# A dense expert network: routing weights broadcast by DMA from device memory, rings of three banks, down projection two pairs behind

## What is computed

```python
fs = _grouped_routing_scores(router_scores)            # zero outside the groups chosen
up = jnp.einsum('td,edh->teh', xt, Wup) + bup
gate = jnp.einsum('td,edh->teh', xt, Wgate) + bgate
h = jax.nn.silu(up) * gate * fs[:, :, None]
out = jnp.einsum('teh,ehd->td', h, Wdown) + fs @ bdown
x = _layernorm(x + out)
```

## Time and profile before

| what | us |
|---|---|
| median of the runs (3 runs, lowest and highest) | 5069.64 (5061.39 to 5078.28) |
| span of the profiled execution, first to last instruction | 5066.8 |
| stage 2, `expert_mlps`: from ScalarE's first instruction to VectorE's first sum with x | 536.0 to 767.7 |
| in it, TensorE busy | 81% of the whole span; in 536 to 767 us 205.0 of 231.0 |

### The profile page before, as it was taken

The page is one execution under the profiler, slowest core; times in us unless marked ns, Lnnn a source line. Parts: engine busy times, 40 slices in busy tenths (PEclk is TensorE's granted clock), DMA queues, the critical chain, the costliest instruction groups (busy, mean ns, idle before and its releaser), DMA issues. The chain is left out here.

```text
span 5066.8 us, 77700 instructions
## 1 busy us (share of the span) xinstructions
PE 4085.0 (81%) x29323; PEld 2224.5 (44%) x29323; DVE 3485.7 (69%) x5453; ACT 2507.2 (49%) x3544; POOL 1378.9 (27%) x1033
## 2 busy tenths in 40 slices
PE   5640696999999999999995995866996767888883
PEld 3630234666666666666652332432443332222232
DVE  5579444777777777777784445766773558888868
ACT  2120243666666666666662223543564344677772
POOL 0000300566666666666664303000000100000000
PEclk5565798999999999999997996987997687999996
DMA  0010001000000000000003106316650333323300
GB/s 19 1 60 0 0 0 51 1 14 1 14 1 14 14 1 14 1 14 1 1 1 130 58 0 150 53 15 102 84 77 4 90 59 62 55 48 53 49 3 9
DMA packets 135603, 167.70 MB, mean 33 GB/s; under 512 B 19498, under 2 KB 108092, under 8 KB 134676
## 3 DMA queue, kind: packets, MB, share of 16 engines
q1 hardware_dynamic: 127540, 146.39, 14.3%
q0 software_dynamic: 6528, 16.42, 1.3%
q10 hardware_dynamic: 1184, 0.12, 0.0%
HBM read 125.31 MB, written 34.55 MB: 32 GB/s over the span
## 5 line engine op out<-in xcount | busy, mean ns | idle before, releaser
L3001 POOL TENSOR_TENSOR arena<-arena 128x512 f32<-128x512 f32 (+1 forms) x768 | 1131.7, 1475 | 692.0 <-ACT arena L2957 638.6
L2452 ACT ACTIVATE arena<-ps 128x1024 f32<-128x1024 f32 (+1 forms) x688 | 703.3, 1023 | 333.7 <-PE ps L2377 323.0
L2470 DVE TENSOR_REDUCE arena<-ps 128x2 f32<-128x826 f32 (+1 forms) x576 | 564.9, 981 | 185.3 <-PE ps L2323 177.5
L3017 DVE TENSOR_TENSOR arena<-arena 128x1024 f32<-128x1024 f32 (+1 forms) x448 | 644.9, 1478 | 13.8 <-ACT arena L2984 13.8
L3039 DVE TENSOR_TENSOR arena<-ps,arena 128x512 f32<-128x512 f32 (+1 forms) x768 | 530.4, 691 | 178.5 <-ACT arena L2951 144.4
L2323 PE MATMUL ps<-arena 48*128 48x413 bf16 (+3 forms) x1920 | 436.4, 334 | 135.9 <-DVE arena L2470 67.2
L2951 ACT ACTIVATE arena<-ps 128x1024 f32<-128x1024 f32 (+1 forms) x448 | 410.3, 960 | 205.1 <-PE ps L2879 197.0
L2863 PE MATMUL ps<-arena 128*128 128x256 f32 (+1 forms) x1664 | 444.0, 392 | 20.5 <-DVE arena L3025 19.2
L2957 ACT ACTIVATE arena<-arena 128x1024 f32<-128x1024 f32 (+1 forms) x448 | 425.0, 992 | 50.7 <-DVE arena L3017 48.2
L2396 PE MATMUL ps<-arena 128*9 128x256 f32 (+2 forms) x5504 | 436.2, 389 | 10.5 <-ACT arena L2440 7.7
L2879 PE MATMUL ps<-arena 64*128 64x256 f32 (+1 forms) x3328 | 427.3, 391 | 5.5 <-ACT arena L2973 1.3
(11 more groups left out here) (647 smaller groups left out, 5810.8 us busy)
## 6 DMA issues: line engine op xcount, KB each, us to landing
arena<-ctx_parts SPq DMA_DIRECT2D x96, 200.1 KB
arena<-ctx_parts SPq DMA_DIRECT2D x192, 100.1 KB
arena<-in_ctx_feat SPq DMA_DIRECT2D x8, 1601.0 KB, 6.4
arena<-in_ctx SPq DMA_DIRECT2D x16, 768.0 KB
arena<-diff_att_stack SPq DMA_DIRECT2D x60, 192.0 KB
ctx_parts<-arena SPq DMA_DIRECT2D x24, 400.2 KB, 3.8
arena<-in_w SPq DMA_DIRECT2D x1, 6416.0 KB, 18.3
arena<-in_ctx_feat SPq DMA_DIRECT2D x8, 800.5 KB
```

The costliest lines, as they stand in the source:

```text
L2452: act.activation(self.prob[0:rows, u % 3, :], self.ps[0:rows, 2 * (u % 2):2 * (u % 2) + 2, :].rearrange("p n c -> p (n c)"), ACT.Exp).then ...
L2470: ins = dve.tensor_reduce(dst[:, :, j // 2], self.ps[:, 4:6, 0:hi - lo], AX.X, ALU.max)
L3001: pool.tensor_tensor(acc[0:rows, u % 2, :], before, sc[0:rows, u % 2, t, :], ALU.add).then_inc(added, 1)
L3017: dve.tensor_tensor(e, e, mb[0:rows, u % 2, None, :].to_broadcast([rows, n, 2 * S]), ALU.subtract).then_inc(sub_done, 1)
```

## The change

It touches only stage 2.

- `expert_scores`: SyncE waits for `mask_ready` and stores `fs` (64 x 2,048 f32, 0.5 MB) to a scratch tensor `fs_rows` in device memory (new line 1038).
- `expert_mlps`: SyncE loads, for each block n and each chunk c of two pairs, the 8 experts' rows of `fs_rows`, each repeated over 32 partitions, into a buffer `share` [128, 16, 512]: four DMAs per chunk (one per 32 partitions, 2 rows of 2 KB for each partition), 128 in all. Those of block 0 wait for the store alone; each later chunk waits until the same chunk of the block before has been read (`gw_ready`).
- The spread product, the spread matrix in the weight slab, GpSimd's splits and ScalarE's pass over the gate bank are gone. VectorE's first instruction is now a `scalar_tensor_tensor`, (gate bank + bias) * share, straight from PSUM.
- Up and gate have rings of three PSUM banks, and `silu`, `gw` and `hid` three buffers (`RING0 = 3`). The down product stands two pairs behind, and two banks (6, 7) take the sums of alternating blocks.
- The loops over n are unrolled; ScalarE copies the sum of block n-1 after the third Silu of block n, and the turn of the first three blocks no longer waits for the copy of the fourth.

```diff
-WEIGHTS[2] = [... ("bdown", E0, D), ("spread", FB, MT0 * P), ...]
+WEIGHTS[2] = [... ("bdown", E0, D), ...]
...
             env.fetch_weights(sp, 3)
+            sp.wait_ge(s["mask_ready"], 1)
+            sp.dma_start(e["fs_rows"], e["fs"][:, :]).then_inc(e["fs_stored"], 16)
...
+        by_place = e["fs_rows"].rearrange("(m q) t -> q m t", q=QE)
+        @block.sync
+        def _(sp):
+            sp.wait_ge(e["fs_stored"], 16)
+            for n in range(N):
+                for c in range(chunks):
+                    if n:
+                        sp.wait_ge(gw_ready, (n - 1) * MT0 + 2 * c + 2)
+                    for q in range(QE):
+                        sp.dma_start(share[q * H0:(q + 1) * H0, 2 * c:2 * c + 2, :],
+                                     by_place[q:q + 1, 2 * c:2 * c + 2, n * BANK:(n + 1) * BANK]
+                                     .to_broadcast([H0, 2, BANK])).then_inc(share_in[c], 16)
...
+            def down(i):
+                n, m = i // MT0, i % MT0
+                pe.wait_ge(hid_ready, i + 1)
+                if m == 0 and n >= 2:
+                    pe.wait_ge(y_copied, n - 1)
+                pe.matmul(ps[:, 6 + n % 2, :], W("wdown")[:, m * D:(m + 1) * D], hid[:, i % RING0, :],
+                          start=(m == 0), stop=False).then_inc(hid_used, 1)
+                if m == MT0 - 1:
+                    pe.matmul(ps[:, 6 + n % 2, :], W("bdown"), e["fs"][:, n * BANK:(n + 1) * BANK], start=False,
+                              stop=True).then_inc(y_ready, 1)
+            for i in range(total):
+                n, m = i // MT0, i % MT0
+                xs = x_feat[:, n * BANK:(n + 1) * BANK]
+                if i >= RING0:
+                    pe.wait_ge(silu_ready, i - RING0 + 1)
+                pe.matmul(ps[:, i % RING0, :], W("wup")[:, m * P:(m + 1) * P], xs, start=True, stop=True
+                          ).then_inc(up_ready, 1)
+                if i >= RING0:
+                    pe.wait_ge(gw_ready, i - RING0 + 1)
+                pe.matmul(ps[:, RING0 + i % RING0, :], W("wgate")[:, m * P:(m + 1) * P], xs, start=True, stop=True
+                          ).then_inc(gate_ready, 1)
+                if i >= 2:
+                    down(i - 2)
+            down(total - 2)
+            down(total - 1)
             for t in range(NT):
+                if t % 4 == 0:
+                    pe.wait_ge(y_copied, t // 4 + 1)
...
+            for i in range(total):
+                n, m = i // MT0, i % MT0
+                act.wait_ge(up_ready, i + 1)
+                if i >= RING0:
+                    act.wait_ge(hid_ready, i - RING0 + 1)
+                act.activation(silu[:, i % RING0, :], ps[:, i % RING0, :], ACT.Silu, bias=W("bup")[:, m:m + 1]
+                               ).then_inc(silu_ready, 1)
+                if m == 2 and n:
+                    take_y(n - 1)
+            take_y(N - 1)
...
+            for i in range(total):
+                n, m, k = i // MT0, i % MT0, i % RING0
+                dve.wait_ge(gate_ready, i + 1)
+                if m % 2 == 0:
+                    dve.wait_ge(share_in[m // 2], (n + 1) * QE * 16)
+                if i >= RING0:
+                    dve.wait_ge(hid_ready, i - RING0 + 1)
+                dve.scalar_tensor_tensor(out=gw[:, k, :], in0=ps[:, RING0 + k, :], scalar=W("bgate")[:, m:m + 1],
+                                         in1=share[:, m, :], op0=ALU.add, op1=ALU.mult).then_inc(gw_ready, 1)
+                dve.wait_ge(gw_ready, i + 1)
+                dve.wait_ge(silu_ready, i + 1)
+                if i >= RING0:
+                    dve.wait_ge(hid_used, i - RING0 + 1)
+                dve.tensor_tensor(hid[:, k, :], silu[:, k, :], gw[:, k, :], ALU.mult).then_inc(hid_ready, 1)
```

More of the change, by code:

```diff
@@ L990, in layout2 @@
     n = np.arange(P)
-    expert = np.arange(E0 * H0) // H0
-    spread = (np.arange(FB)[:, None] % EB == expert[None, :] % EB).astype(f)
     half = n // E0
@@ L1205, in expert_mlps @@
         st = Stage(env, ctx, "mlp0")
[L1206 to L1209, removed]
-        y = st.sb("y", [P, T])
[L1211 to L1215, removed]
+        N = T // BANK
+        total, chunks = N * MT0, MT0 // 2
+        silu = st.sb("silu", [P, RING0, BANK])
+        gw = st.sb("gw", [P, RING0, BANK])
+        hid = st.sb("hid", [P, RING0, BANK])
+        share = st.sb("share", [P, MT0, BANK])
+        y = st.sb("y", [P, T])
+        share_in = [st.sem(f"share{c}_in") for c in range(chunks)]
+        up_ready, gate_ready, silu_ready = st.sem("up_ready"), st.sem("gate_ready"), st.sem("silu_ready")
         gw_ready, hid_ready, hid_used = st.sem("gw_ready"), st.sem("hid_ready"), st.sem("hid_used")
@@ L1222, in _ @@
         @block.tensor
         def _(pe):
[L1224 to L1241, removed]
-                    pe.matmul(ps[:, 4 + m % 2, :], spread_h[:, m * P:(m + 1) * P],
-                              fs_parts[:, m * P // H0 // EB, bass.ds(n * BANK, BANK)], start=True, stop=True
-                              ).then_inc(up_ready, 1)
-                    if m:
-                        down(n, m - 1)
-                down(n, MT0 - 1)
-                pe.matmul(ps[:, 6, :], W("bdown"), e["fs"][:, bass.ds(n * BANK, BANK)], start=False, stop=True
-                          ).then_inc(y_ready, 1)
@@ L1254, in _ @@
                     ins.then_inc(turned, 1)
+            pe.wait_ge(y_copied, N)
             norm.run_pe(pe, HIGH)
[L1257 to L1281 removed]
@@ L1283, in _, with take_y @@
         @block.scalar
         def _(act):
[L1286 to L1296 removed]
+            def take_y(n):
+                act.wait_ge(y_ready, n + 1)
+                act.activation(y[:, n * BANK:(n + 1) * BANK], ps[:, 6 + n % 2, :], ACT.Copy).then_inc(y_copied, 1)
@@ L1334, in stage2 @@
         e["W"] = Pack(e["wt"], WEIGHTS[2])
+        e["fs_rows"] = env.nc.dram_tensor("fs_rows", (E0, T), F32, kind="Internal").ap()
+        e["fs_stored"] = st.sem("fs_stored")
         e["sorted"] = lambda buf: buf[1]
```

58 lines of the change are left out of this document (6 added, 52 removed).

## The result

| | before | changed |
|---|---|---|
| median, the runs of the first comparison (4 each), us | 5068.27 | 4996.19 |
| lowest to highest | 5061.39 to 5078.28 | 4985.95 to 5004.92 |
| ratio, 95% interval | | 0.9861 (0.9841 to 0.9880) |
| span of the profiled execution | 5066.8 | 4984.1 |
| time of the profiled execution | not listed | 4985.95 |

The kernel is 72 us faster by these medians. Inside the stage the trace agrees with the forecast to a microsecond; the profiled spans differ by 82.7 us, of which the stage holds 59.0.

A forecast was written before the change was run, and what follows sets the result against it. TensorE's list bounds the expert stage: 168.6 us of products + 2.5 of half clock + 0.7 at the end = 171.8 us against 231.7, a gain of 59.9. 5069.6 - 59.9 = 5010 us, range 5000 to 5036.

The forecast's parts named there:

- What bounds the stage: Expert stage: TensorE's list and its holes set the time; 171.8 us after the change against 231.7 before.
- Spread product: TensorE in the expert loop: dropping 64 spread products of 0.22 us each saves 14 us.
- Holes in the pairs: TensorE's waits for late hid in the expert loop: gone, since the new distance gives 5.2 us for a 0.69 + 0.72 chain.
- Clock: TensorE at the stage's start: 5 us at half speed, costing 2.5 us, then granted clock 1.00.
- VectorE's new instruction: Expert loop: 690 ns at the median, taken from another stage; VectorE needs 1.41 us per pair of 2.58.
- Transfers: Loads of fs_rows: must come at 102 GB/s for TensorE, and are hidden behind it.
- I take the first two: Rate for the share loads: 309 and 285 GB/s from other transfers, rather than 123 at worst.
- The rival by which the transfers come one after the other: Share loads not overlapping set the stage: 128 x 2.3 = 294 us; slower case, 5125 us at 60 GB/s, chance 0.06.
- First share: Start of the stage: first chunk lands by 541 us, slack about 1.5 us, hidden narrowly.
- GpSimd's moved instruction: 7.23 us moved to a later stage, ahead of a 51.23 us wait for ScalarE: hidden; uncovered it costs 7.2.
- 5069.6 - 59.9: Whole kernel: median of the runs before, less the expert stage's gain, gives 5010 us.
- the gain can't pass 63: Lower end of the range, 5000 us: TensorE's 168.6 us are a floor, so the gain is capped.

The follow-up runs named there:

- distinct: Changed kernel with each partition loading rows of its own from the weight slab, routing weights left out; expert stage 388.4 us against 388.5.
- after: The changed kernel itself, as first profiled against the kernel before: median 4996.19 us, ratio 0.9861, expert stage 388.5 us.
- warm: Changed kernel plus 19 unread f32 products on TensorE ahead of its wait for fs; expert stage 386.1 us, median 4988.67 us.
- double: Changed kernel with every transfer of shares made twice, the second into an unread spare buffer; expert stage 431.0 us against 388.5.

## Why the prediction was right and where it was wrong

- **What bounds the stage: right.** TensorE's list and its holes; 196 products at 0.86 us are 168.6 us, and the stage with start and end took 172.7 against a sum of 171.8. Around each bias product the starts are up to 0.2 us further apart than 0.86, 0.35 per block (42.45 against 42.1), and the half clock was a little shorter. The gain in the stage was forecast as 59.9 and is 59.0 by the profile that the sum was made against; by the later profiles of the kernel before it is 55.6 to 58.1, so the agreement to a microsecond is in part luck.
- **Spread product, 14 us: right**, 14.4.
- **Holes in the pairs: right in the sum, not in what cured them.** The change's rings and distance, which I had given as the reason that `hid` is in time, are worth 2.2 us. The pass over the gate bank that ScalarE lost, together with the earlier start of its Silu, is worth 18.4, and I had costed the pass at "nothing beyond the holes counted", which is true only because the sum rebuilt the list and did not ask where the holes came from. The third product of the stage starts 16.7 us earlier (538.48 against 555.86, of which 0.7 lie ahead of the stage). If 2.2, 18.4, 14.4 and 16.7 may be added, some 7 us of the 59 are left for the ends of blocks and of the stage; of these only the order at the end of a block was put back alone, and it was worth 0.4.
- **Clock: right.** 4.3 us at half speed instead of 5, then 1.00.
- **VectorE's new instruction: a little under-sized**, 0.75 us instead of 0.69; hidden. The instruction of the earlier trace rows has a constant for its scalar where this one has a column of biases; whether that is the reason wasn't tried.
- **Transfers: hidden, but with less room than said.** The step "I take the first two" (309 and 285 GB/s) failed in size: full DMA engines gave 153 to 199. Against 102 that is a margin of 1.5 at the lowest, and the doubled transfers, which ask for 204, made the stage 431.0 us long, where 430 had been worked out from 158. The Trainium skill, DMA: Bandwidth & Descriptors, section Latency and other measured facts, gives 103 GB/s for copies with row pitches of 4 MiB and 8 MiB. No run here has such a pitch; the loads with a repeated row were slower than those of `distinct`, but by less than that. The rival by which the transfers come one after the other is refuted: a transfer of 128 KB took 4.1 us to land at the median, and yet every 5.2 us brought four. The Trainium skill, on the same page, section Anatomy of one DMA, fits the time of one DMA issued from GpSimd. The loads here are issued from SyncE, and the trace disagrees with taking that time for each DMA of a queue in turn.
- **First share: right and narrow.** Landed by 540.23 (541 forecast); the slack was 0.6 us, where 1.5 was said.
- **GpSimd's moved instruction: right**, hidden.
- **The total: wrong.** Two steps failed. "5069.6 - 59.9" took the median of three runs as the level of the kernel before; 72 runs have a median of 5058.9, so the base was 10.7 us too high. From that base the same sum gives 4999.0, and the changed kernel's 27 runs have 4997.2. The first comparison has the same three runs and one more (5068.27), so its 72 us are too large by about as much. That these few runs lay high was chance as far as the later ones tell. The second is the lower end of the range, "the gain can't pass 63": a floor for the stage was used as a floor for the time. From 5069.6 it leads to 5006.6, so the range left 6.6 us for the scatter of both kernels. The kernel before had shown 8 us to either side of its median, and both the base and the result wander so, with a last attention stage that takes 781 to 815 us as chance has it. A lower end at 5010 - 16 = 4994 would have held the result.

## What to carry to other kernels

Where one engine's list is the bound, write down the new list and multiply; that gave the stage to 1 us against one profile of the kernel before, and to 4 us against another, but to know what an edit is worth, put parts back one at a time, since here the longer rings and distance gave 2.2 us, and a dropped pass on an engine with time to spare, together with the earlier start of the pass beside it, 18.4. Such a pass still lengthens the chain to the engine that has none. Take the level of the whole from as many runs as there are, and put the spread of the parts not touched on both sides of the forecast.

## What the runs showed of the hardware

- Loads that repeat one source row over 32 partitions (2 rows of 2 KB each) ran at 153 to 199 GB/s with full DMA engines (after); loads with rows of its own for each partition, from another tensor, ran at 224 to 233 (distinct).
- Behind 19 us of products of 512 columns, TensorE's clock fell to half 2.3 us into 16 products of one column (warm), though the engine had stood for only 0.85 us ahead of them; waits of up to 2.7 us between products of 512 columns (double) left it at 1.00 in most stretches (0.91 from 640 to 660 us).
- The same program's last attention stage took 780.6, 785.5, 788.4 and 803.3 us in four profiles of the changed kernel, with TensorE's granted clock at half for about 0, 0, 3 and 23 us of it. The stretches at half are 3 to 14 us long and lie at places that differ from execution to execution.
